# Down product by output quarters sorted by knots, with per-segment sums, in a decoder layer built from spline weights

## The chip, the cores and the metric

One NeuronCore of a Trainium2 chip runs the whole layer as one program. The metric is the device time of one execution in microseconds, the median over runs. The engines are TensorE (PE; its weight loads are shown as PEld), VectorE (DVE), ScalarE (ACT), GpSimd (POOL) and SyncE (SP, which issues DMAs here). TensorE has two clock levels, 1.2 and 2.4 GHz; a granted clock of 1.00 is 2.4 GHz.

## The reference

`x` is (8, 256, 512): 8 batches of 256 tokens. The layer is

```
x = layernorm(x + attention(x))           # 16 heads of 32, softmax, low-rank down/up per head
x = layernorm(x + x * scan(ctx * ctx))    # per head r = decay * r + ctx^2 along the tokens
gate, up = x @ gate_w.T, x @ up_w.T       # gate_w, up_w: (2048, 512)
x = layernorm(x + (silu(gate) * up) @ down_w.T)   # down_w: (512, 2048)
```

Each of the three feed-forward weights is a Catmull-Rom spline over a flat index: 8134 control points over 1,048,576 elements, so a knot falls every 128.9 elements. Between two knots the weight is a cubic polynomial of the flat index. Each output row of `down_w` has 2048 elements and thus some 16 knots.

## The kernel before, in words

**Precision.** Matmul operands are mostly fp32r. A value is split into a high part and a remainder (`hi`, `lo`), and one product is three matmuls: high x high, high x low, low x high (helper `three`, lines 303 to 305). Where an operand is plain f32, one call shows in the trace as two records.

**Attention part**, batch by batch (`pe_batch`, `act_batch`, `dve_batch`, `pool_batch`). For each of four groups `m` of four heads: `pe_s` makes the scores (line 478; each head uses 32 rows of the array and its own bank), DVE takes the maxima (`dve_max`, line 821), ACT the exponentials with their sums (`act_exp`, line 665), PE transposes them (`pe_t`, line 490), DVE and ACT copy them to SBUF (`probsT`, line 835), DVE inverts the sums and widens them (`dve_inverse`, lines 827 and 830), PE transposes those (`pe_r`, line 498), and `pe_pv` multiplies with V (line 512; each head writes its own 32 partitions). Between these PE does projections of the next batch. The order on PE is `pe_pv(m)`, then `pe_s(m + 1)`. The recurrence is a scan on DVE (`dve_scan`, line 896), after the copies of group 2, or in the last batch in two halves before the inverses of groups 2 and 3. `pe_extra` puts transposes of spline coefficients (batches 1 to 3) and jobs (batches 4 to 7) in between.

**Jobs.** A job makes one tile of weights from spline coefficients: `pe_job` (line 1096) multiplies makers (powers of the position) with coefficients for the piece before and the piece after a knot, ACT copies the first (`act_job`, line 1105), DVE overwrites it by mask with the second (`dve_job`, line 1117), ACT rounds the high part (line 1124), and GpSimd or DVE makes the low part (`pool_job_lo`, line 1132, `dve_job_lo`, line 1139). Sixteen jobs make gate and up in a basis of a few features per 128 inputs; 32 jobs of two matmuls (128 rows, 256 columns) make the whole down weight, `dn[g]`. Makers and masks come by GpSimd's DMA queue. The first `AHEAD_JOBS` run before the feed-forward part.

**Feed-forward part.** Four blocks `n` of 512 tokens; in each, 8 steps `g` (256 of the 2048 hidden units each), j = 0, 1 (128 units each). The inputs are first turned to features (`pe_xt`, transposes, line 1165; `pe_features`, line 1191; then ACT and DVE split them and SP's queue spreads them by group, line 1220). These run ahead for the next block as "turns" through the single bank `F`, three places in each step. `pe_gate_up` makes `G` and `U` (three matmuls of 512 columns each); `act_silu` (line 1356) reads `G`, `dve_hm` (line 1398) multiplies with `U`, `act_hh` (line 1369) rounds and `dve_hl` (line 1402) takes the remainder. Banks `G`, `U` and the tile `hidden` are single. `pe_down` multiplies the hidden values of the step before with `dn[g]`: for each of four tiles of 128 tokens, two `j` times three matmuls, summed over all 8 steps in banks 0 to 3. The order on PE in a step is written out by hand:

```
gate/up 0, turn 0, down 0, fill 0, down 1, fill 1, turn 1,
gate/up 1, fill 2, down 2, fill 3, turn 2, down 3
```

where the fills are the remaining jobs, in block 0 alone. After step 7 DVE adds the residual (`dve_add`, line 1408) and takes statistics (lines 1412, 1594), GpSimd the reciprocal root (lines 1638, 1640), DVE normalizes (`dve_out`, line 1426), and GpSimd issues the output DMAs (line 1482). ACT and DVE do their work of a step in a fixed order as well (`act_step`, `dve_step`): every engine takes its instructions in program order.

## Time and profile before

| | us |
|---|---|
| median of 3 runs (684.74 to 684.94) | 684.91 |
| the profiled execution | 685.51 |
| its span, first to last instruction | 683.7 |
| PE busy (4312 matmuls) | 656.8 (96%) |
| DVE busy | 449.5 (66%) |
| ACT busy | 347.7 (51%) |
| POOL busy | 294.3 (43%) |

The attention part ends at about 367, the first gate/up matmul starts at 376.7, the last matmul at 672.99. The duration of a single matmul includes the way through the array and overlaps with the next one; the spacing of the starts is what it costs PE. Idle time is that of the engine before the instruction named, and what released it.

### The profile page before, as it was taken

How to read it: one execution, taken by the hardware profiler on the slowest of the kernel's cores; microseconds unless marked ns; L12 is line 12 of the kernel's file. 1: busy time of each engine (PE TensorE's matmuls, PEld its weight loads, DVE VectorE, ACT ScalarE, POOL GpSimd, SP SyncE). 2: the span in 40 equal slices, each digit the busy share in tenths (PEclk: the TensorE clock that was granted, in tenths of full speed). 3: DMA queues.
4: the chain of work that ended last, by engine and by line, in shares of the span. 5: the costliest groups of instructions: out<-in, count | busy, mean ns of one | idle time of the engine just before them, and what ended most of it. 6: DMA issues, size and time to landing. Idle time of an engine off the chain costs nothing.

```text
span 683.7 us, 12025 instructions
## 1 busy us (share of the span) xinstructions
PE 656.8 (96%) x4312; PEld 533.8 (78%) x4312; DVE 449.5 (66%) x826; ACT 347.7 (51%) x1002; POOL 294.3 (43%) x351
## 2 busy tenths in 40 slices
PE   9999999999999999999988799999999999999993
PEld 9597887878888788788865577888888888888883
DVE  3567687698686877878778688666544555354434
ACT  5566546637466565656667556552334233333230
POOL 1764486886638767594674836100100001000103
PEclk9999999999999999999999999999999999999997
DMA  9621020030220311121112672741193317340301
GB/s 329 221 80 62 1 87 7 2 125 1 94 62 2 133 52 32 63 72 41 40 65 47 159 173 72 210 105 40 35 239 78 81 32 198 72 101 0 124 1 61
DMA packets 22010, 58.06 MB, mean 85 GB/s; under 512 B 4032, under 2 KB 7232, under 8 KB 21056
## 3 DMA queue, kind: packets, MB, share of 16 engines
q1 hardware_dynamic: 16720, 44.45, 22.5%
q0 software_dynamic: 4944, 12.32, 5.9%
q8 instruction: 35, 0.57, 0.3%
...
## 4 chain that ended last, share of the span: by engine, by line
PE 78%; DVE 12%; ACT 6%; issue 2%; POOL 1%; DVEq 0%; POOLq 0%; ACTq 0%
PE bank L303 19%; PE bank L305 18%; PE bank L304 18%; PE bank L490 6%; ACT probs L665 5%; PE bank L478 4%; DVE recurrence_T L896 4%; PE bank L512 4%; DVE minus_max L821 3%; PE bank L1191 2%; PE bank L1096 2%; DVE probsT L835 2%; PE bank L529 1%; PE bank L316 1%; PE bank L498 1%
## 5 line engine op out<-in xcount | busy, mean ns | idle before, releaser
L665 ACT ACTIVATE probs<-bank,minus_max 128x256 f32<-128x256 f32 x256 | 117.3, 486 | 23.8 <-DVE minus_max L821 23.8
L303 PE MATMUL bank<-down,hidden_hi_lo 128*128 128x512 f32 x256 | 100.7, 393 | 1.5 <-DVE hidden_hi_lo L1402 1.5
L305 PE MATMUL bank<-down,hidden_hi_lo 128*128 128x512 f32 x256 | 100.5, 392 | 0.0
L304 PE MATMUL bank<-down,hidden_hi_lo 128*128 128x512 f32 x256 | 100.0, 391 | 0.0
L821 DVE TENSOR_REDUCE minus_max<-bank 128x2 f32<-128x512 f32 x128 | 79.3, 681 | 16.3 <-PE bank L478 16.3
L1398 DVE TENSOR_TENSOR hidden<-bank,silu 128x512 f32<-128x512 f32 x64 | 44.1, 689 | 60.9 <-PE bank L305 58.9
L1356 ACT ACTIVATE silu<-bank 128x512 f32<-128x512 f32 x64 | 38.3, 598 | 82.2 <-PE bank L305 81.3
L1402 DVE TENSOR_TENSOR hidden_hi_lo<-hidden,hidden_hi_lo 128x512 fp32r<-128x512 f32 x64 | 45.5, 711 | 40.9 <-ACT hidden_hi_lo L1369 40.8
L490 PE MATMUL bank<-ident,probs 128*128 128x128 f32 x512 | 65.5, 275 | 6.2 <-ACT probs L665 5.9
L1476 POOL TENSOR_TENSOR ffn_var_eps<-ffn_mean_var,constants 128x4 f32<-128x4 f32 x3 | 0.6, 196 | 156.5 <-DVE ffn_mean_var L1418 156.5
L490 PEld LDWEIGHTS bank<-ident,probs 128*128 128x128 f32 x512 | 56.6, 141 | 14.2 <-ACT probs L665 12.0
L1369 ACT CAST hidden_hi_lo<-hidden 128x512 fp32r<-128x512 f32 x64 | 39.8, 622 | 52.3 <-DVE hidden L1398 52.3
L835 DVE COPY probsT<-bank 128x512 f32<-128x512 f32 x96 | 60.1, 680 | 4.8 <-PE bank L490 4.7
L303 PEld LDWEIGHTS bank<-down,hidden_hi_lo 128*128 128x128 f32 x256 | 48.1, 188 | 11.5 <-DVE hidden_hi_lo L1402 1.9
L305 PEld LDWEIGHTS bank<-down,hidden_hi_lo 128*128 128x128 f32 x256 | 48.0, 188 | 10.3
L665 ACT ACTIVATION_READ_ACCUMULATOR probs<-bank,minus_max 128x1 f32 x256 | 55.9, 219 | 0.0
L304 PEld LDWEIGHTS bank<-down,hidden_hi_lo 128*128 128x128 f32 x256 | 48.1, 188 | 9.7
L303 PE MATMUL bank<-xT_hi_lo,wq_hi 128*128 128x256 f32 x128 | 38.7, 303 | 1.1 <-DVE spline_coef_T_down L773 0.4
L303 PE MATMUL bank<-xT_hi_lo,wk_hi 128*128 128x256 f32 x128 | 38.9, 304 | 0.0
L512 PE MATMUL bank<-probsT,V 128*32 128x256 f32 x512 | 36.8, 385 | 0.4 <-ACT inverse_by_query L680 0.4
L478 PE MATMUL bank<-k_heads,q_heads 32*128 32x256 f32 x512 | 36.7, 400 | 0.0
L305 PE MATMUL bank<-xT_hi_lo,wq_lo 128*128 128x256 f32 x128 | 36.1, 282 | 0.0
...
## 6 DMA issues: line engine op xcount, KB each, us to landing
features_by_group<-features_by_cell SPq DMA_DIRECT2D x128, 128.0 KB, 2.4
...
```

The costliest lines, as they stand in the source:

```text
L303: nc.tensor.matmul(out, wh, xh, start=first, stop=False)
L304: nc.tensor.matmul(out, wh, xl, start=False, stop=False)
L305: return nc.tensor.matmul(out, wl, xh, start=False, stop=last)
L478: last = nc.tensor.matmul(S[g][:, t * T:(t + 1) * T], qk[0][at, m, t * P:(t + 1) * P], qk[1][at, m, :], start=True, stop=True)
L490: last = nc.tensor.transpose(S[g][:, kt * T + t * P:kt * T + (t + 1) * P], probs[:, g, t, kt * P:(kt + 1) * P], ident[:])
L512: last = nc.tensor.matmul(MI[g * DH:(g + 1) * DH, 0:T], V[:, kt, h * DH:(h + 1) * DH], probsT[:, g, kt, :], start=kt == 0, stop=kt == TT - 1)
L665: inc(nc.scalar.activation(probs[:, g, t, :], S[g][:, t * T:(t + 1) * T], ACT.Exp, bias=nmax[:, g, t:t + 1], accum_out=rsum[:, t, g:g + 1] ...
L821: inc(nc.vector.tensor_reduce(nmax[:, g, :], S[g][:].rearrange("p (t k) -> p t k", t=TT), AX.X, ALU.max, negate=True), "max")
L835: inc(nc.vector.tensor_copy(probsT[:, g, :, :], S[g][:].rearrange("p (k t) -> p k t", k=2)), "ptv")
L1369: inc(nc.scalar.copy(hid[:, g % 2, 0, j, :], hm[:]), "hh")
L1398: inc(nc.vector.tensor_tensor(hm[:], U[:], sg[:], ALU.mult), "hm")
L1402: inc(nc.vector.tensor_tensor(hid[:, g % 2, 1, j, :], hm[:], hid[:, g % 2, 0, j, :].bitcast(F32), ALU.subtract), "hl")
```

## The change

The down product is taken the other way round, with the outputs on the partitions of the banks and 512 tokens as columns. The 512 outputs are sorted by where their knots fall and cut into 4 quarters of 128; the 2048 hidden units are cut into 64 segments between knots, 16 for each quarter. For a quarter, the 512 hidden units of its own segments, where its knots lie, are multiplied with exact weights (`pe_raw`: 64 units of quarter 2 * pair on rows 0 to 63 and 64 of the next on rows 64 to 127, each with its own bank; one more such tile for two units that were moved between quarters). All other weights are cubic over each segment, so four sums per segment (`pe_moments`: of the hidden values times 1, k, k^2, k^3) times four coefficients give their share (`pe_polynomials`). The quarters' results are split and brought back to token rows and to the outputs' order by matmuls with a 0/1 matrix (`pe_place`). Steps are now `st`: steps 0 to 3 take hidden units of quarters 0 and 1, steps 4 to 7 of 2 and 3.

The down weights take 13 jobs instead of 32; a job is now 16 calls (the one for the moved units 32) in plain f32 with 64 stationary columns, 128 moving columns, into upper or lower partitions of banks 2 and 3 in turn. Four of them run ahead, nine in steps 0 to 3 of block 0. Turns, fills and the last steps get new places.

In the attention part the scores of the next group go ahead of the product with V, the maxima ahead of `dve_y`, `act_yh` into the middle of the exponentials; the widening of the inverse goes from DVE to ACT; the scan goes whole to before the inverse of group 2, and in the last batch behind the attention. At the end of the program ACT normalizes (a third small GpSimd step makes -mean * rstd) and SP issues the output DMAs.

The core of the diff (left out: the tables made on the host, buffers, semaphores, and edits that follow from these):

```diff
         if proj:
             pe_k(pe, nb, 1, rest)
         pe_extra(pe, b, 2)
+
+        pe_s(pe, b, 3)
         pe_pv(pe, b, 2)
-
-        pe_s(pe, b, 3)
         if proj:
             pe_v0(pe, nb)
             pe_v1(pe, nb, range(0, 2))
...
             pe.wait_ge(s_mkg[g % 2], 16 * (g // 2 + 1))
             by = [(mk_gu[g % 2][:, piece * P:(piece + 1) * P], splD[w][:, g, :]) for piece in range(2)]
         else:
-            g, k = divmod(i - 2 * NG, 2 * JT)
-            j, hf = divmod(k, 2)
-            pe.wait_ge(s_mkd[g % 2], 16 * (g // 2 + 1))
-            by = [(mk_dn[g % 2][:, j * P:(j + 1) * P], downD[:, j, piece, hf * GROUP:(hf + 1) * GROUP]) for piece in range(2)]
+            k = i - 2 * NG
+            pe.wait_ge(s_mkd[k % 4], 16 * (k // 4 + 1))
+            mk = mk_dn[k % 4][:].rearrange("p (c b h m) -> p c b h m", c=2, b=2, h=2).bitcast(F32)
+            for piece in range(2):
+                for cb in range(2):
+                    for b in range(2):
+                        q, terms = job_terms(k, cb, b, piece)
+                        o = out[b * PART:(b + 1) * PART, piece * GROUP + cb * P:piece * GROUP + (cb + 1) * P]
+                        for n, (of, coef) in enumerate(terms):
+                            for h in range(2):
+                                last = nc.tensor.matmul(o, mk[:, of, b, h, :], downD[:, h, coef, q * P:(q + 1) * P].bitcast(F32),
+                                                        start=n == h == 0, stop=h == 1 and n == len(terms) - 1)
+            inc(last, "w")
...
+    def pe_moments(pe, n, st):
+        pair, pr = divmod(st, Q)
+        pe.wait_ge(s["hl"], JT * (STEPS * n + st) + JT)
+        if pr == 0:
+            wait(pe, "mol", 2 * n + pair)
+            if n == st == 0:
+                wait(pe, "ws", AHEAD_JOBS)
+                pe.wait_ge(s["seg"], 16)
+        for h in range(2):
+            for j in range(JT):
+                last = nc.tensor.matmul(Mo[:], by_segment[:, JT * st + j, :], hid[:, st % 2, h, j, :],
+                                        start=pr == h == j == 0, stop=pr == Q - 1 and h == j == 1)
+        if pr == Q - 1:
+            inc(last, "mo")
+
+    def pe_raw(pe, n, st):
+        pair, pr = divmod(st, Q)
+        pe.wait_ge(s["hl"], JT * (STEPS * n + st) + JT)
+        if n == 0:
+            if st < 4:
+                pe.wait_ge(s["wl"], 2 * NG + st + 1)
+            else:
+                pe.wait_ge(s["wld"], STEPS - 3 if st == MOVED_STEP else st - 3)
+        for b in range(2):
+            q = 2 * pair + b
+            if pr == 0 and n == 0:
+                if pair == 0:
+                    wait(pe, "r1", 2 * B)
+                else:
+                    pe.wait_ge(s["ws"], NJOB)
+                    wait(pe, "rs1", 2 * B)
+            elif pr == 0:
+                wait(pe, "add", BT * (n - 1) + q + 1)
         for j in range(JT):
-            last = three(Dn[t][:], [hid[:, g % 2, h, j, t * P:(t + 1) * P] for h in range(2)], [dn[g][:, h, j, :] for h in range(2)],
-                         g == 0 and j == 0, g == NG - 1 and j == JT - 1)
-        if g == NG - 1:
-            inc(last, "d")
-        elif t == BT - 1:
-            inc(last, "hused")
-
-    OWN = {(1, 1): 4, (1, 2): 5, (2, 0): 6, (2, 1): 7}
-    AHEAD = {(2, 2): 0, (3, 0): 1, (3, 1): 2, (3, 2): 3, (4, 0): 4, (4, 1): 5, (5, 0): 6, (5, 1): 7,
-             (6, 2): 8, (7, 0): 9, (7, 1): 10, (7, 2): 11}
...
+            for k, (lo_w, lo_h) in enumerate(((0, 0), (0, 1), (1, 0))):
+                for b in range(2):
+                    rows_ = slice(b * PART, (b + 1) * PART)
+                    last = nc.tensor.matmul(Dn[2 * pair + b][:], raw[st][rows_, lo_w, j * P:(j + 1) * P],
+                                            hid[rows_, st % 2, lo_h, j, :], start=pr == j == k == 0, stop=False)
+        if st == MOVED_STEP:
+            for lo_w, lo_h in ((0, 0), (0, 1), (1, 0)):
+                last = nc.tensor.matmul(Dn[1][:], raw[STEPS][0:PART, lo_w, 0:P], hid[0:PART, st % 2, lo_h, 0, :],
+                                        start=False, stop=False)
+        inc(last, "hused")
+
+    def pe_polynomials(pe, n, pair, quarters_):
+        pe.wait_ge(s["mol"], 2 * n + pair + 1)
+        if n == 0:
+            wait(pe, "wld", STEPS + 1 - 4 + 2 * pair + 2)
+        for q in quarters_:
+            last = three(Dn[q][:], [by_poly[:, pair, h, q * P:(q + 1) * P] for h in range(2)], [mom[:, pair, h, :] for h in range(2)],
+                         False, pair == 1)
+            inc(last, "d" if pair else "kap")
+
+    def pe_place(pe, n, t):
+        wait(pe, "yll", Q * n + Q)
+        if n == t == 0:
+            pe.wait_ge(s["place"], 16)
+        for q in range(Q):
+            for h in range(2):
+                last = nc.tensor.matmul(Dn[t][:], yq[:, q, h, t * P:(t + 1) * P], places[:, q, :],
+                                        start=q == h == 0, stop=q == Q - 1 and h == 1)
+        inc(last, "pm")
+
+    OWN = {(0, 0): 4, (0, 1): 5, (0, 2): 6, (1, 0): 7}
+    AHEAD = {(1, 2): 0, (2, 0): 1, (2, 1): 2, (2, 2): 3, (3, 0): 4, (3, 1): 5, (3, 2): 6, (4, 0): 7,
+             (7, 0): 8, (7, 1): 9, (7, 2): 10, (8, 0): 11}
...
+    def turn_of(n, st, at):
+
+        if n == 0 and (st, at) in OWN:
+            return 0, BT + OWN[st, at]
+        if n and (STEPS + st, at) in AHEAD:
+            return n, AHEAD[STEPS + st, at]
+        if n < NB - 1 and (st, at) in AHEAD:
+            return n + 1, AHEAD[st, at]
+        return None
+
...
+    FILL = {0: (4, 5), 1: (6, 7), 2: (8, 9), 3: (10, 11, 12)}
+
+    def job_of(n, st, k):
+
+        return 2 * NG + FILL[st][k] if n == 0 and st in FILL and k < len(FILL[st]) else None
+
...
-    def pe_step(pe, n, g):
-        prev = before(n, g)
-        pe_gate_up(pe, n, g, 0)
-        pe_turn(pe, n, g, 0)
-        pe_down(pe, prev, 0)
-        pe_fill(pe, n, g, 0)
-        pe_down(pe, prev, 1)
+    def pe_step(pe, n, st):
+        prev = before(n, st)
+        pe_gate_up(pe, n, st, 0)
+        pe_turn(pe, n, st, 0)
+        if n and st == 1:
+            for t in range(BT):
+                pe_place(pe, n - 1, t)
         if prev:
-            pe_fill(pe, n, g, 1)
-        pe_turn(pe, n, g, 1)
-        pe_gate_up(pe, n, g, 1)
-        pe_fill(pe, n, g, 2 if prev else 1)
-        pe_down(pe, prev, 2)
-        pe_fill(pe, n, g, 3)
-        pe_turn(pe, n, g, 2)
-        pe_down(pe, prev, 3)
+            pe_moments(pe, *prev)
+            pe_fill(pe, n, st, 0)
+            pe_raw(pe, *prev)
+        else:
+            pe_fill(pe, n, st, 0)
+        pe_turn(pe, n, st, 1)
+        pe_fill(pe, n, st, 1)
+        pe_gate_up(pe, n, st, 1)
+        pe_fill(pe, n, st, 2)
+        if n and st == 0:
+            pe_polynomials(pe, n - 1, 1, range(Q))
+        if st == 6:
+            pe_polynomials(pe, n, 0, range(Q))
+        pe_turn(pe, n, st, 2)
 
...
-    def act_step(act, n, g):
-        act_silu(act, n, g, 0)
...
+    def act_step(act, n, st):
+        prev = before(n, st)
+        if n and st == 1:
+            for q in range(2):
+                act_outs(act, n - 1, q)
+        act_silu(act, n, st, 0)
+        if n and st == 1:
+            for q in range(2, Q):
+                act_outs(act, n - 1, q)
+        act_hh(act, n, st, 0)
+        act_turn(act, n, st, 0)
+        if prev and prev[1] % Q == Q - 1:
+            act_moments(act, prev[0], prev[1] // Q)
+        act_fill(act, n, st, 0)
+        act_turn(act, n, st, 1)
+        act_fill(act, n, st, 1)
+        act_fill_hi(act, n, st, 0)
+        act_silu(act, n, st, 1)
+        act_fill_hi(act, n, st, 1)
+        act_hh(act, n, st, 1)
+        act_fill(act, n, st, 2)
+        act_fill_hi(act, n, st, 2)
+        act_turn(act, n, st, 2)
 
...
+    def dve_outs(dve, n, q):
+        dve.wait_ge(s["yhh"], Q * n + q + 1)
+        inc(nc.vector.tensor_tensor(yq[:, q, 1, :], Dn[q][:], yq[:, q, 0, :].bitcast(F32), ALU.subtract), "yll")
+
     def dve_add(dve, n, t):
         if t == 0:
             dve.wait_ge(s["fres"], 16 * n + 16)
-        dve.wait_ge(s["d"], BT * n + t + 1)
+        dve.wait_ge(s["pm"], BT * n + t + 1)
         inc(nc.vector.tensor_tensor(res[:, t, :], Dn[t][:], res[:, t, :], ALU.add), "add")
 
...
             pe_o(pe, B - 1, 1)
             pe.wait_ge(s["ws"], 2 * NG + 2)
             pe_job(pe, 2 * NG + 2, X)
+            pe_rs(pe, B - 1, 0)
+            pe_rs(pe, B - 1, 1)
+            pe.wait_ge(s["ws"], 2 * NG + 3)
+            pe_job(pe, 2 * NG + 3, X)
             for n in range(NB):
-                for g in range(NG):
-                    pe_step(pe, n, g)
+                for st in range(STEPS):
+                    pe_step(pe, n, st)
+            pe_moments(pe, NB - 1, STEPS - 1)
+            pe_raw(pe, NB - 1, STEPS - 1)
+            pe_polynomials(pe, NB - 1, 1, range(Q))
             for t in range(BT):
-                pe_down(pe, (NB - 1, NG - 1), t)
+                pe_place(pe, NB - 1, t)
 
...
```

`dve_step` mirrors `act_step`. In `dve_batch` the calls are moved thus (in `act_batch` the calls of `act_yh` for groups 0 to 2 go):

```diff
         dve_extra(dve, b, 0)
         if post:
             dve_stats(dve, b - 1, 0)
         dve_inverse(dve, b, 1)
         dve_heads(dve, b, 1)
 
+        dve_max(dve, b, 2)
         dve_y(dve, b, 1)
-        dve_max(dve, b, 2)
         dve_extra(dve, b, 1)
-        if not proj:
-            dve_scan(dve, b, range(2))
+        if proj:
+            dve_scan(dve, b)
         dve_inverse(dve, b, 2)
         dve_heads(dve, b, 2)
-        if proj:
-            dve_scan(dve, b, range(KT))
-        else:
+
+        dve_max(dve, b, 3)
+        dve_y(dve, b, 2)
+        if not proj:
             dve_x2l(dve, 0, 0, B_)
             dve_x2l(dve, 0, 1, C_)
-
-        dve_y(dve, b, 2)
-        dve_max(dve, b, 3)
         dve_extra(dve, b, 2)
-        if post:
+        if post and proj:
             dve_size(dve, b - 1)
-        if not proj:
-            dve_scan(dve, b, range(2, KT))
         dve_inverse(dve, b, 3)
         dve_heads(dve, b, 3)
         if not proj:
             dve_x2l(dve, 0, 2, B_)
             dve_x2l(dve, 0, 3, C_)
+            dve_size(dve, b - 1)
         dve_y(dve, b, 3)
...
```

## Rows read from the trace of the kernel before

**Rows 1.** Stretches: us, busy us by engine, granted clock, DMA share, GB/s.

```profile
24.00:361.00 337.00, 327.92 (x2771) 265.88 (x2770) 255.15 (x479) 204.03 (x720) 226.74 (x248) 1.00 0.17 56
...
367.40:376.70 9.30, 9.28 (x46) 7.45 (x47) 6.50 (x15) 5.37 (x13) 2.73 (x6) 1.00 0.44 99
376.70:458.50 81.80, 77.70 (x364) 61.78 (x363) 61.48 (x121) 48.63 (x108) 33.69 (x43) 1.00 0.54 141
458.50:530.20 71.70, 71.70 (x322) 58.59 (x321) 37.03 (x62) 26.17 (x44) 4.01 (x7) 1.00 0.40 102
...
601.80:673.20 71.40, 71.40 (x313) 58.34 (x311) 32.88 (x58) 19.54 (x32) 5.20 (x11) 1.00 0.17 48
673.20:683.80 10.60, 0.18 (x1) 0.00 (x0) 4.16 (x9) 0.00 (x0) 4.65 (x9) 0.66 0.27 99
```

**Rows 2.** Matmul groups by form, 376.7 to 673.3: busy us, mean ns.

```profile
L303 PE MATMUL bank<-down,hidden_hi_lo 128*128 128x512 f32 x256 | 100.7, 393 | 1.5 <-DVE hidden_hi_lo L1402 1.5
...
L1096 PE MATMUL bank<-spline_coef_T_down,makers_out 128*128 128x256 f32 x60 | 12.5, 290 | 1.4 <-DVE weights_now L1117 1.4
```

**Rows 3.** One step of block 2 in order of time: start, us, engine.

```profile
588.46 0.60 ACT L1356 ACTIVATE silu<-bank 128x512 f32<-128x512 f32 x1 [2.08 <-PE bank L305]
...
588.72 0.40 PE L305 MATMUL bank<-features_by_group,weights_lo_up 128*128 128x512 f32 x1
...
589.15 0.69 DVE L1398 TENSOR_TENSOR hidden<-bank,silu 128x512 f32<-128x512 f32 x1 [2.06 <-PE bank L305]
...
589.88 0.62 ACT L1369 CAST hidden_hi_lo<-hidden 128x512 fp32r<-128x512 f32 x1 [0.82 <-DVE hidden L1398]
...
590.33 0.61 PE L1191 MATMUL bank<-x2T_hi_lo,moments 128*128 128x512 f32 x2
590.53 0.69 DVE L1402 TENSOR_TENSOR hidden_hi_lo<-hidden,hidden_hi_lo 128x512 fp32r<-128x512 f32 x1 [0.69 <-ACT hidden_hi_lo L1369]
...
590.98 0.59 ACT L1206 CAST features_by_cell<-bank 128x512 fp32r<-128x512 f32 x1 [0.48 <-PE bank L1191]
...
591.60 0.69 DVE L1211 TENSOR_TENSOR features_by_cell<-bank,features_by_cell 128x512 fp32r<-128x512 f32 x1 [0.37 <-ACT features_by_cell L1206]
```

**Rows 4.** Tiled matmuls between untiled ones, order of time, PE.

```profile
249.61 0.48 PE L1096 MATMUL bank<-spline_coef_T_gate,makers_hidden 128*128 128x256 f32 x2
250.02 1.12 PE L512 MATMUL bank<-probsT,V 128*32 128x256 f32 x16
251.07 1.15 PE L478 MATMUL bank<-k_heads,q_heads 32*128 32x256 f32 x16
252.15 0.39 PE L303 MATMUL bank<-xT_hi_lo,wq_hi 128*128 128x256 f32 x1
```

**Rows 5.** Plain f32 matmuls, untiled, order of time, PE.

```profile
10.98 3.74 PE L341 MATMUL bank<-recurrence_T,spline_coef_rows 128*128 128x128 f32 x32
14.47 0.36 PE L303 MATMUL bank<-xT_hi_lo,wq_hi 128*128 128x256 f32 x1
```

**Rows 6.** Steps 0 and 1 of block 0, order of time, PE.

```profile
383.61 0.40 PE L305 MATMUL bank<-features_by_group,weights_lo_up 128*128 128x512 f32 x1
385.49 0.49 PE L303 MATMUL bank<-down,hidden_hi_lo 128*128 128x512 f32 x1 [1.49 <-DVE hidden_hi_lo L1402]
```

**Rows 7.** Waits of PE in attention: total us, times, longest.

```profile
PE bank L490 <- ACT probs L665: 5.9, 19, 0.8
```

**Rows 8.** DVE in batch 5, order of time.

```profile
267.42 0.20 DVE L827 RECIPROCAL row_sum_inverse<-row_sum 128x8 f32<-128x8 f32 x1 [1.67 <-ACT probs L665]
...
270.26 4.88 DVE L896 TENSOR_TENSOR_SCAN recurrence_T<-decay,ctx_squared_T 128x256 f32<-128x256 f32 x4
```

**Rows 9.** The end, order of time.

```profile
672.99 0.39 PE L305 MATMUL bank<-down,hidden_hi_lo 128*128 128x512 f32 x1
...
674.89 0.68 DVE L1408 TENSOR_TENSOR x_residual<-bank,x_residual 128x512 f32<-128x512 f32 x1
...
677.65 0.55 DVE L1426 TENSOR_SCALAR x_residual<-x_residual,ffn_mean_var,ffn_rstd 128x512 f32<-128x512 f32 x1 [0.70 <-POOL ffn_rstd L1640]
```

599 lines of the change are left out of this document (356 added, 243 removed).

## The prediction

> **What bounds the kernel now.** I read the stretches first, then the matmul groups, one step in order of time, the waits, and the end. TensorE (PE) is the bound: of 337 us of attention it idles 9, in blocks 1 to 3 of the feed-forward part nothing, and the granted clock is 1.00 up to the end [rows 1]. Block 3 is the ruler: 71.40 us for 313 matmuls of 512 columns, back to back, 0.228 us each [rows 1]. Elsewhere PE waits in the first steps of block 0 (4.1 us of 81.8 [rows 1], the longest 1.49 us for the low half of the hidden values [rows 6]), on softmax in attention (5.9 us [rows 7]), and for the 10.6 us after the last matmul, when only VectorE, GpSimd and the output DMAs work [rows 1, 9]. So a change pays only by what it takes from PE's list, and costs whatever it puts there, waits included.
>
> **Step chain.** The chain behind each hidden tile, from the start s of the last `up` matmul (588.72) [rows 3]: silu starts at s-0.26, `hidden` s+0.43, high half s+1.16, low half s+1.81, ready at about s+2.53; silu releases `G` at s+0.39, `hidden` releases `U` at s+1.17. A turn (features or transposes through the one bank `F`) frees the bank 1.96 us after it begins: matmuls at 590.33, copy at 590.98, subtraction 591.60 to 592.29, if both engines are free. Before, two output tiles of the down product (12 matmuls, 2.7 us) stand between a step's second gate/up and the next step's first, and again behind that first; they hide this chain.
>
> **The change, PE's list per normal block.** Gone: 192 down matmuls. Added: 32 for `pe_moments`, 24 for `pe_polynomials`, 32 for `pe_place`, 3 for the moved units, and 96 half-height matmuls in `pe_raw`. These last alternate between rows 0 to 63 and 64 to 127 and between two banks. Row and column tiles at work [rows 4]: scores (32 rows, four tiles) and probabilities times V (32 columns, four tiles) do 16 records each in 1.05 and 1.08 us, against 32 records of 128 columns in 3.49 us untiled [rows 5], that is 0.109 each, 0.218 for 256 columns. Four tiles thus run nearly side by side. I count a pair of half-height matmuls as one of 0.228. fp32r in row tiles is not in this trace; the other end is no overlap, 0.456. So the list falls from 304 to 251 slots, 53 less, 12.1 us a block: 48.3 us in all.
>
> **Switches.** From the first untiled matmul of 249.61 to that of 252.15 pass 2.54 us. Its two L1096 matmuls take 0.24, the eight groups of four 8 x 0.218 = 1.74; 0.56 is left for three changes of tiling, 0.18 each [rows 4]. Every `pe_raw` has two, 32 of them: 64 x 0.18 = 11.5 us; the jobs (column tiles) add about 14 changes, 2.5 us. Bounds: nothing to 0.3 each (all of one group's latency).
>
> **New waits.** In the new `pe_step` all moments and raw work lies between gate/up 0 and gate/up 1; between gate/up 1 and the next step's moments lie only the 6 matmuls of the next gate/up and the turns. (a) No turns there (4 to 5, 5 to 6 in each block, and three more in block 3): PE reaches `G` at s+0.23, waits to s+0.39; `U` at s+1.08, waits to s+1.17; moments at s+1.85, wait to s+2.53. 0.9 us, eleven times: 10 us. (b) A turn before and one after that gate/up: the first turn's copy stands behind the high half on ScalarE and its subtraction behind the low half on VectorE, so bank `F` is free only at s+3.1, where PE asks at s+2.05. 1.05 us, twelve times (less with a fill between, more often shared with 0.2 in the turn before): 12 us. (c) `pe_place` wants all four quarters split high and low: after the last polynomial PE has 6 matmuls (1.4 us), the split of quarter 3 queues behind silu and `hidden` of the new step and ends 3.5 us after it: 2.1 us, three times. (d) In step 3 of blocks 1 and 2 the turn stands behind four statistics (2.4 us) of `dve_out_stats`: 2.1 us each. (e) At the end the low half (2.3) and the last split (1.6) are bare. Behind a waiting PE nothing else can go, and ScalarE and VectorE then wait for PE.
>
> **Jobs.** `pe_job` of the outputs was 2 matmuls of 256 columns, about 0.24 us (60 such records in the blocks [rows 2]). Now it is 16 calls in plain f32, 32 records of 128 columns at 0.109 [rows 5], in two column tiles; side by side 1.74, with start and drain 1.95 us; one after another 3.5. What decides between the ends [rows 4]: there too a tile's own records come one after the other and the four tiles still run together. Twelve such jobs, one of double length, for 32 old ones.
>
> **Blocks.** Blocks 1 and 2: 203 full matmuls 46.3, 48 pairs 10.9, 16 transposes 1.7, 16 switches 2.9, waits 2.1 + 2.1 + 1.8 + 4.2 = 10.2: 72.0, with gate/up's slower 0.231 about 72.3, against 71.7. Block 0: 161 matmuls 36.7, 42 pairs 9.6, transposes 1.7, ten job lengths 19.5, 28 switches 5.0, waits 7: 79.5; I add 1.5, since its job waits before were never quite what the chain says: 81.0 against 81.8. Block 3 up to the last matmul, with two blocks' worth of placing and three of polynomials' groups: 237 matmuls 54.0, 54 pairs 12.3, switches 3.2, waits 2.1 + 4.5 + 2.3 + 1.6 = 10.5, and 1 for gate/up's pace: 81.0 against 71.4. Sum: -0.8 + 1.2 + 9.6 = +10.
>
> **Bridge** (367.4 to 376.7, 9.3 us [rows 1]): four jobs with switches, 4 x 2.3 = 9.2, for three of 0.24 to 0.5; the rest stays, and the scan of the last batch (4.8 us [rows 8]) is hidden by the output projection. +8.
>
> **Attention.** Scores move ahead of the product with V, so the maxima begin 1.05 us earlier; the scan goes ahead of the inverse. PE's softmax waits (5.9 [rows 7]) may go. But the scan starts near 265.1 instead of 270.26 and lasts 4.8 (270.26 to 275.07), where VectorE had 1.67 us free [rows 8]: the inverse, ready at 267.42, comes at 269.9, and ScalarE's wide copy and PE's `pe_r` wait 0.6 us for it. In batches 0 to 6 that gives back most: -3 in all, with the projection's wait at batch 0. In batch 7 no scan is left and two phases shorten: -3.3. Together -6.3; bounds -12 (all 9.1 of PE's idle time in the stretch, and some 2 to 3 behind it) and +3 (nothing gained, 0.6 lost in five batches).
>
> **End.** Before: last matmul 672.99, span 683.7, 10.7 us; VectorE lagged, its last add came 1.9 us behind the matmul, and GpSimd issued four DMAs at the end [rows 9]. After: placing (8 matmuls, 1.8 us) paces the adds, the add follows at +0.42, statistics and mean +1.45, GpSimd's three small steps 1.3, ScalarE 0.9 with its wait, SyncE's DMA and the end about 3.5 (before, 5.5 from the last normalization to the end with four DMAs issued in a row by GpSimd): 7.7. -3.
>
> Sum: -6.3 + 8 + 10 - 3 = +8.7 on the span 683.7, 692.4; 1.8 us lie around the span (685.51), and the median of the runs is 0.6 below that execution: **693.5 us**. Makers, masks and `places` come over GpSimd's queue a step or more ahead; `pool_norm2` of batch 6 delays makers 8 to 11 by 7 us, used from step 2, 18 us on: nothing. The extra evacuations on ScalarE and VectorE (six of 0.6 to 0.7 us a block) fit: both are under 55% busy in block 1 [rows 1]. Features' DMAs keep their distance of two steps.
>
> **The order of tiles.** For the jobs it matters in which order tiles may start [rows 4]. There, 16 records of 0.218 in four column tiles take 1.05 us, though each call is two records on its own tile. Were every record to start in the program's order, the second record of one call would hold back the next tile's first, and the product with V would need 9 x 0.218 = 1.96 us. It does not; so I let the two tiles of a job run side by side. The Trainium skill ("TensorE: Matmul & The Clock Gate", on packing small matmuls, what overlaps and what doesn't) says instead that matmuls start and end strictly in program order. By that rule the sum would be that of rival 2; the trace speaks against it.
>
> **Rivals.**
> 1. *Changing the tiling costs nothing where PE's queue is full* (it is paid within a wait). 86 switches less: -15.4, 678. For it: switches beside waits may share them. Against: [rows 4], where the queue was full and 0.56 us are missing. It decides from 0.08 us a switch downward.
> 2. *Job records in strict order.* A job is four times eight records, four on one tile and then four on the other; in strict order only the last of the one lies beside the first of the other, 6 x 0.109 instead of 4, so 2.7 in place of 1.95, fourteen lengths: +10.5, 704. No overlap at all: 3.5, +21.7, 715. For it: four records in a row on one tile are deeper than the two of [rows 4].
> 3. *Row pairs don't overlap in fp32r*: 192 x 0.228 less 3 us of waits hidden, +41, 734. Against: [rows 4], where the scores write four banks at once at a column every two cycles each, the same total.
> 4. *The waits at step ends are smaller*, or attention gives its whole 12 us: 684 to 689, no change or a little slower.
>
> **Chances.** My forecast 0.55, its own range 688 to 700. Rival 1 0.20, rival 2 0.12 and 0.04, rival 3 0.04, rival 4 0.05. A measurement tells 0.2% (1.4 us) from no change. Faster: rival 1 and a little of 4 and of attention, 0.25; within, 0.07; slower 0.68. Range 679 to 706: it leaves out no overlap, about 0.1, and the edge of rival 1.
>
> **What would show it.** Blocks 1 and 2 of 72 us in place of 71.7, with PE busy about 90% instead of 100%. PE idle before `moments` behind the low half (0.7 us, eleven times), before turns behind `features_by_cell` or `x2T` (1 us), before placing 2 us. A raw burst of 12 records in 1.4 to 1.6 us; 2.7 would be rival 3. A job of 32 records in 2.0; 3.5 would be rival 2. Weight loads "issue" 0.3 us at each change of tiling. In attention the transposes of head group 3 without waits and `pe_r` of group 2 with 0.6. The prediction fails if switches are free, if the jobs don't pair, or if the attention part shortens by over 9 us.

## The result, and the profile after

The changed kernel takes **706.03 us** (median; 699.7 to 707.1), the kernel before 684.92 us on the same chip: a ratio of 1.0287, 95% interval 1.0225 to 1.0349. It is slower, by 21.1 us where 8.6 were forecast. The profiled execution took 705.22 us, its span is 703.3 us.

The same stretches as in [rows 1], now of the kernel after: us, busy us (and instructions) of TensorE (PE), its weight loads, VectorE (DVE), ScalarE (ACT), GpSimd (POOL), then the granted clock, DMA share and GB/s. They are attention, the bridge, blocks 0 to 3, and the end.

```profile
24.00:356.20 332.20, 325.09 (x2802) 268.62 (x2801) 232.13 (x452) 218.86 (x766) 229.03 (x254) 0.99 0.19 62
356.20:381.00 24.80, 20.27 (x168) 16.26 (x169) 12.12 (x24) 6.45 (x15) 10.24 (x15) 0.86 0.57 136
381.00:462.50 81.50, 75.12 (x584) 56.08 (x582) 44.16 (x78) 32.82 (x66) 31.73 (x43) 1.00 0.40 102
462.50:538.80 76.30, 67.60 (x316) 47.49 (x315) 39.97 (x68) 28.06 (x50) 5.96 (x9) 0.98 0.49 128
538.80:612.40 73.60, 66.02 (x317) 46.45 (x316) 40.07 (x68) 27.95 (x50) 3.98 (x7) 1.00 0.36 94
612.40:697.10 84.70, 76.31 (x346) 52.67 (x344) 42.64 (x73) 27.81 (x48) 6.12 (x14) 0.98 0.18 50
697.10:703.30 6.20, 0.00 (x0) 0.00 (x0) 1.57 (x3) 1.78 (x3) 1.95 (x6) 0.85 0.34 128
```

Against [rows 1]: attention ends 11.2 us earlier (its first feature matmul starts at 356.2 instead of 367.4), the bridge is 15.5 us longer, block 0 0.3 shorter, blocks 1 and 2 4.7 and 2.0 longer, block 3 13.1 longer, and from the end of the last matmul to the end of the span pass 6.2 us instead of 10.3. Together +19.6 on the span. The reader sees two things at once. PE was busy for all of blocks 1 to 3 before; now it is busy for about 90%. And the granted clock, 1.00 before in every stretch but the end, is now below 1.00 in four of the six stretches ahead of the end.

The waits of PE in the four blocks, total us, times, longest; before there were none in blocks 1 to 3:

```profile
PE bank L1346 <- DVE features_by_cell L1366: 10.1, 11, 1.7
PE bank L1463 <- DVE outs_hi_lo L1627: 7.4, 4, 2.0
PE bank L1413 <- DVE hidden_hi_lo L1619: 6.7, 12, 2.2
PE bank L1320 <- DVE x2T_hi_lo L1333: 3.1, 3, 1.0
PE bank L1346 <- DVE x2T_hi_lo L1333: 2.2, 3, 0.9
```

L1346 and L1320 are turns (features, transposes), L1463 is the placing, L1413 the moments. These are waits (a) to (e) of the prediction. With one of 1.0 us for the tables of a job (makers_out) there are 34, 30.5 us in all; the prediction had 37.9.

One step of block 3 in order of time, PE, start and us:

```profile
667.69 1.20 PE L1413 MATMUL bank<-hidden_hi_lo,by_segment 128*128 128x512 f32 x4 [0.42 <-DVE hidden_hi_lo L1619]
668.81 1.66 PE L1440 MATMUL bank<-hidden_hi_lo,down_raw 64*128 64x512 f32 x12
670.41 0.50 PE L440 MATMUL bank<-features_by_group,spline_coef_T_gate 128*128 128x512 f32 x1
670.75 0.39 PE L441 MATMUL bank<-features_by_group,spline_coef_T_gate 128*128 128x512 f32 x1
670.98 0.40 PE L442 MATMUL bank<-features_by_group,weights_lo_gate 128*128 128x512 f32 x1
```

Twelve half-height matmuls take 1.60 us from their first to the next gate matmul: the pairs do run side by side. A change of tiling has two parts here: the first matmul of the new kind comes 0.32 us after the last of the old (670.41 is 0.32 behind the last pair) instead of 0.23, and the one behind it 0.34 (670.41 to 670.75) instead of 0.23. Together 0.20 us. The weight loads of the same three matmuls show where the second part comes from:

```profile
670.41 0.19 PEld L440 LDWEIGHTS bank<-features_by_group,spline_coef_T_gate 128*128 128x128 f32 x1 [0.37 <-issue]
670.51 0.19 PEld L441 LDWEIGHTS bank<-features_by_group,spline_coef_T_gate 128*128 128x128 f32 x1
670.75 0.19 PEld L442 LDWEIGHTS bank<-features_by_group,weights_lo_gate 128*128 128x128 f32 x1
```

In a full stream the load of the next matmul begins together with the matmul before it (670.75). Here the first matmul's own load begins at 670.41, with the matmul, and the second's only at 670.51, 0.10 us late. The Trainium skill names a cause for the first part ("TensorEngine Tiling (Array Packing)", Tiling Modes): a change of the tiling mode, other than of the tile, makes TensorE drain first. The trace gives the price; whether the array is empty at 670.41 it cannot tell, since the ends of matmuls are modelled.

The placing of block 0's outputs, at 475.59 in order of time, and under it the windows of two half-clock stretches:

```profile
473.22 0.39 PE L442 MATMUL bank<-features_by_group,weights_lo_up 128*128 128x512 f32 x1
475.59 5.76 PE L1463 MATMUL bank<-spline_coef_T_down,outs_hi_lo 128*128 128x512 f32 x17 [1.99 <-DVE outs_hi_lo L1627]
```

```profile
476.10:479.50 3.40, 3.40 (x9) 2.66 (x9) 0.51 (x2) 0.00 (x0) 0.00 (x0) 0.51 1.03 216
626.30:629.70 3.40, 3.40 (x10) 2.62 (x9) 0.69 (x1) 0.00 (x0) 0.00 (x0) 0.51 0.00 0
```

PE stands still for 2 us, and right behind it the clock is at its lower level (1.2 of 2.4 GHz) for 3.4 us, in which about 8 matmuls start instead of 15: 1.6 us lost. It happened behind two of the three placings between blocks; the third, a wait of 1.98 us at 551.9, was followed by none, nor was the longest wait for the low half, 2.16 us at 682.4. Three more such stretches begin at 349.9 us, in attention's last batch, behind a wait of 2.5 us for transposed inputs, and at 360.1 and 377.2 us in the bridge, the one behind a wait of 1.95, the other within one of 2.54. So, from 24 us on, five of the seven waits of 1.9 us and more brought one.

### The profile page after: what moved, and what is told of

Read it like the earlier page. It is cut to its first block, busy times and chain, and to the rows that moved or that the text cites. A ratio compares the mean times of both kernels' runs of the same rounds, so it can differ in the third digit from the quotient of the medians.

```text
span 703.3 us, 12746 instructions
## 1 busy us (share of the span) xinstructions
PE 652.1 (93%) x4676; PEld 507.4 (72%) x4676; DVE 421.6 (60%) x775; ACT 356.2 (51%) x1024; POOL 297.8 (42%) x364
## 4 chain that ended last, share of the span: by engine, by line
PE 79%; DVE 12%; ACT 5%; DMA 2%; issue 1%; POOL 1%; DVEq 0%; ACTq 0%; POOLq 0%
PE bank L440 13%; PE bank L442 12%; PE bank L441 11%; PE bank L627 8%; PE bank L1440 7%; PE bank L615 5%; PE bank L1463 5%; PE bank L1413 4%; PE bank L649 4%; PE bank L1249 3%; DVE hidden L1615 3%; DVE hidden_hi_lo L1619 3%; ACT hidden_hi_lo L1574 3%; PE bank L1346 2%; ACT probs L804 1%
## 5 line engine op out<-in xcount | busy, mean ns | idle before, releaser
L804 ACT ACTIVATE probs<-bank,minus_max 128x256 f32<-128x256 f32 x256 | 118.8, 487 | 39.7 <-DVE minus_max L966 39.5
L627 PE MATMUL bank<-ident,probs 128*128 128x128 f32 x512 | 63.1, 277 | 1.1 <-ACT probs L804 1.1
L627 PEld LDWEIGHTS bank<-ident,probs 128*128 128x128 f32 x512 | 58.6, 143 | 4.2 <-ACT probs L804 1.8
L1440 PE MATMUL bank<-hidden_hi_lo,down_raw 64*128 64x512 f32 x384 | 53.1, 408 | 0.0
L1440 PEld LDWEIGHTS bank<-hidden_hi_lo,down_raw 64*128 64x128 f32 x384 | 33.7, 184 | 16.6 <-issue 10.8
L1059 POOL TENSOR_TENSOR yT_lo<-heads_out,yT_hi 128x256 fp32r<-128x256 f32 x24 | 19.9, 831 | 57.6 <-ACT yT_hi L812 57.6
L1413 PE MATMUL bank<-hidden_hi_lo,by_segment 128*128 128x512 f32 x128 | 36.2, 404 | 6.7 <-DVE hidden_hi_lo L1619 6.7
L1463 PE MATMUL bank<-spline_coef_T_down,outs_hi_lo 128*128 128x512 f32 x128 | 33.5, 424 | 7.4 <-DVE outs_hi_lo L1627 7.4
L1346 PE MATMUL bank<-x2T_hi_lo,moments 128*128 128x512 f32 x64 | 23.0, 445 | 15.0 <-DVE features_by_cell L1366 10.1
L1463 PEld LDWEIGHTS bank<-spline_coef_T_down,outs_hi_lo 128*128 128x128 f32 x128 | 26.0, 205 | 14.8 <-DVE outs_hi_lo L1627 9.0
L442 PE MATMUL bank<-xT_hi_lo,wq_lo 128*128 128x256 f32 x128 | 36.2, 283 | 0.0
```

Of the source, the lines that this page charges most:

```text
L442: return nc.tensor.matmul(out, wl, xh, start=False, stop=last)
L627: last = nc.tensor.transpose(S[g][:, kt * T + t * P:kt * T + (t + 1) * P], probs[:, g, t, kt * P:(kt + 1) * P], ident[:])
L804: inc(nc.scalar.activation(probs[:, g, t, :], S[g][:, t * T:(t + 1) * T], ACT.Exp, bias=nmax[:, g, t:t + 1], accum_out=rsum[:, t, g:g + 1] ...
L1413: last = nc.tensor.matmul(Mo[:], by_segment[:, JT * st + j, :], hid[:, st % 2, h, j, :], start=pr == h == j == 0, stop=pr == Q - 1 and h = ...
L1440: last = nc.tensor.matmul(Dn[2 * pair + b][:], raw[st][rows_, lo_w, j * P:(j + 1) * P], hid[rows_, st % 2, lo_h, j, :], start=pr == j == k ...
L1463: last = nc.tensor.matmul(Dn[t][:], yq[:, q, h, t * P:(t + 1) * P], places[:, q, :], start=q == h == 0, stop=q == Q - 1 and h == 1)
```

## Experiments

All times are medians of four executions; ratios are to the kernel before, run on the same chip (its medians there: 685.0, 686.0 and 685.1 us). The change itself was not run beside them: what is said to be less or more than the change compares with the 706.03 above, so differences of 1 us mean nothing there. Where intervals of ratios overlap, the profiled executions decide.

**1. The attention part alone.** The kernel before with the change's attention edits; the last batch's scan and transposes of the recurrence behind the output projection, as in the change.

```
before:  pe_pv(b, m-1); pe_s(b, m)          now:  pe_s(b, m); pe_pv(b, m-1)
before:  dve_y; dve_max; inverse; scan      now:  dve_max; dve_y; scan; inverse
bridge:  + dve_scan(B-1) behind job 16, pe_rs(B-1) behind the last job, pool_scaled(B-2) ahead of the jobs' low parts
```

> The kernel before with the change's attention part alone (scores ahead of the product with V, the evictions and the scan in their new places); its feed-forward part and its jobs are those of before. Theory: the attention part ends some 11 us earlier (356.2 instead of 367.4 us in the trace of after) and nothing behind it takes that back, since the jobs of the bridge are short again: 673 to 677 us, a ratio near 0.985. Rival: the last batch's scan and the size chain, now behind the attention part, hold up the bridge, and at least half of it is given back: 679 to 684 us.

677.84 us, ratio 0.9892 (0.9877 to 0.9907): faster than before by 7.2 us. Attention ends at 356.1 us, as in the change, and the bridge takes 13.0 us instead of 9.3. So some 4 of the 11.3 us are given back there: the scan, the size chain and the transposes now lie in the bridge, and a half-clock stretch of 3.4 us begins at 360.0. Another begins at 349.8, as in the change; the kernel before has neither. The gain in the whole is nearly the 6.3 of the forecast, and the time lies between what the two theories named.

**2. Twice the changes of tiling.** The change, with moments and row pairs each cut in two.

```
-  moments(4 matmuls); raw(12)
+  moments(h=0: 2); raw(j=0: 6); moments(h=1: 2); raw(j=1: 6)
```

> After, with the moments of a step cut in two: two matmuls, the first half of the row pairs, the other two matmuls, the second half. The same matmuls in number and size, 62 more changes between whole matmuls and row pairs. Theory (a change of tiling costs 0.18 to 0.2 us of TensorE): +11 to +13 us, a ratio of 1.016 to 1.018. Rival (a change of tiling is free and what the trace shows there belongs to waits): within 1 us of after.

715.43 us, ratio 1.0442 (1.0421 to 1.0463). In the profiled executions the span grows by 9.3 us, with four half-clock stretches ahead of the end against five, so by 10.9 at the same clock. The edit makes 64 more changes of tiling, two in each of 32 steps (143 in the blocks instead of 79), not the 62 I had counted: 0.17 us for each. PE's waits in the blocks shrink by 1.6 us, so some of the price falls into them; a change with no wait beside it costs the 0.20 above. Second matmuls that come 0.31 to 0.37 us after the first rise from 127 to 186. The growth is just under the 11 to 13 of the theory; the rival (free) falls, and with it rival 1 of the prediction.

**3. Another order within a step.**

```
-  gate/up 0; turn 0; [place]; moments(prev); raw(prev); turn 1; gate/up 1; [polynomials]; turn 2
+  gate/up 0; moments(prev); turn 0; gate/up 1; turn 1; [place]; raw(prev); [polynomials]; turn 2
```

The copies and subtractions of turn 1 and the four additions follow behind the second hidden tile on ScalarE and VectorE; the splits of the moments go ahead of turn 0's.

> After, with the work of a step in another order: the moments directly behind the first gate/up, the placing, the row pairs and one turn behind the second gate/up, so that each wait has other matmuls ahead of it. The same matmuls, the same number of changes of tiling. Theory (a large part of the loss in the blocks is waiting that the order causes; by the durations of the trace the waits shrink from 17 to some 2 us, and the drops of the clock behind them go too): 15 to 22 us less than after, 684 to 691 us. Rival (the loss is in the switches and the exposed weight loads, which stay): at most 5 us less, 701 us or more.

681.44 us, ratio 0.9949 (0.9931 to 0.9968): 24.6 us less than the change with the same matmuls and 75 changes of tiling in the blocks in place of 79, and now faster than before. Its blocks:

```profile
378.20:461.60 83.40, 75.59 (x583) 59.39 (x582) 46.45 (x79) 34.16 (x67) 33.88 (x45) 0.96 0.40 104
461.60:530.20 68.60, 65.20 (x316) 48.11 (x315) 40.00 (x67) 28.57 (x50) 4.13 (x7) 0.98 0.54 142
530.20:599.10 68.90, 65.28 (x316) 47.86 (x315) 39.90 (x67) 28.35 (x50) 3.99 (x7) 0.98 0.38 100
599.10:672.90 73.80, 71.24 (x346) 52.73 (x344) 42.10 (x72) 27.65 (x47) 6.18 (x14) 1.00 0.19 55
```

Blocks 1 and 2 fall below the 71.7 of before. The waits for hidden_hi_lo go from 6.7 us (12 times) to 0.6 (once), those of the placing from 7.4 to 1.4. Block 0 is 1.9 us longer than in the change: a wait of 3.7 us for the tables of the last job, one of 2.4 for a turn, and a half-clock stretch with each. The drops of the clock did not go, as the theory had it: there are five ahead of the end, as in the change. So the 24 us between the two profiled executions (680.87 at a mean clock of 0.985, 705.22 at 0.987) are not the clock's; most of them are waits. Two of the five come in blocks 1 and 2, where no wait is longer than 1.02 us, behind two such waits 2 us apart:

```profile
495.46 0.50 PE L440 MATMUL bank<-features_by_group,spline_coef_T_up 128*128 128x512 f32 x1 [0.92 <-DVE hidden L1614]
497.44 0.73 PE L1346 MATMUL bank<-x2T_hi_lo,moments 128*128 128x512 f32 x2 [1.00 <-DVE features_by_cell L1366]
```

```profile
498.20:501.70 3.50, 3.50 (x14) 2.38 (x15) 1.29 (x2) 0.93 (x2) 0.00 (x0) 0.51 0.00 0
```

The other is at 566.5 us, behind waits of 0.93 and 1.02.

**4 and 5. One piece of that order each.** First only the row pairs behind the second gate/up, then only the placing (with the row pairs of that step and the additions).

```
4:  -  moments(prev); raw(prev); turn 1; gate/up 1        5:  -  [place]; moments; raw; turn 1; gate/up 1
    +  moments(prev); turn 1; gate/up 1; raw(prev)            +  moments; turn 1; gate/up 1; [place]; raw   (step 1 only)
```

> After, with one thing of the new order alone: the row pairs of a step behind the second gate/up instead of ahead of it. Theory (the wait for the second gate/up and the one for the low part at the step's end shrink when matmuls stand between them; the placing still waits): 6 to 10 us less than after, 696 to 700 us. Rival (the gain of the new order lies in the moments, turns and placing): within 3 us of after, 703 us or more.

699.29 us, ratio 1.0200 (1.0161 to 1.0238; the top of it touches the change's interval): 6.7 us less than the change. The waits for the low half fall from 6.7 to 0.6 us, but the turns' for features_by_cell rise from 10 to 14, and the clock is worse (mean 0.979, with half-clock stretches from 377 us on at 377.7, 428.9, 500.6, 551.8 and 579.1 us, the third of double length).

> After, with the placing alone (and the row pairs that wait for it, and the four additions on VectorE) behind the second gate/up of step 1 instead of behind the first, three times in the kernel. Theory (2.0 us of waiting each, and the clock's drop behind two of them, go once other matmuls stand ahead): 6 to 9 us less than after, 697 to 700 us. Rival (the chain of the second gate/up is then bare, since nothing stands between the two gate/up groups but the moments): 1 to 3 us less.

690.12 us, ratio 1.0065 (1.0048 to 1.0082): 15.9 us less than the change by the medians, twice what I expected. The spans of the profiled executions differ by 14.5, of which 12.6 lie in blocks 1, 2 and 3:

```profile
460.60:530.90 70.30, 65.57 (x317) 46.38 (x316) 40.10 (x68) 28.29 (x50) 5.92 (x9) 1.00 0.53 138
530.90:601.40 70.50, 65.61 (x316) 46.41 (x315) 40.04 (x68) 28.28 (x50) 3.98 (x7) 1.00 0.37 98
601.40:682.60 81.20, 75.24 (x346) 52.77 (x344) 42.60 (x73) 27.95 (x48) 6.12 (x14) 0.98 0.18 52
```

6.0, 3.1 and 3.5 us less. Step 1 of each gave 3.9, 2.3 and 4.3 (the wait of 2.0, the restart, and the half clock where there was one), step 2 0.9, 0.9 and 0.7 (a wait less), and step 7 of block 1 1.1; step 7 of block 3 lost 1.5 to a half-clock stretch at the wait of 2.16, which brought none in the change. The bridge, which the edit does not touch, is 1.6 us shorter, because its wait of 2.54 brought no half-clock stretch this time. That part is luck. The piece that costs most in the change is still where it places. The two pieces together give 22.6 of the 24.6 us of experiment 3; its other moves (the moments, turn 1) no run tests alone.

**6. PE kept busy during one wait.** The change, with eight matmuls more, whose result is not used, ahead of the placing between blocks.

```
+  wait(pe, "fl", NFT * (n + 1))
+  for k in range(8): nc.tensor.matmul(F[:], splD[0][:, 0, 0:P], feat[:, 0, 0, :], ...)
   for t in range(BT): pe_place(pe, n - 1, t)
```

> After, with eight more matmuls of 512 columns (8 x 0.228 = 1.8 us; their result is not used) in each of blocks 1 to 3 ahead of the placing, where TensorE stands still for 2 us. Theory (the drops of the granted clock come from TensorE standing still): the stretches at the half level at 476 and 626 us are gone and the rest stays, 1 to 4 us less than after, 702 to 705 us. Rival (the drops have nothing to do with the wait): they stay, and the time is that of after or up to 1 us more.

701.83 us, ratio 1.0245 (1.0210 to 1.0281). That interval and the change's overlap, so the time alone shows no gain; the trace is the evidence. The same two places:

```profile
474.00:482.00 8.00, 8.00 (x39) 6.35 (x39) 2.77 (x4) 0.00 (x0) 0.00 (x0) 1.00 0.59 121
612.00:630.00 18.00, 17.83 (x86) 13.93 (x84) 8.88 (x14) 4.49 (x9) 0.00 (x0) 1.00 0.27 60
```

No stretch at the half level is left between 362 us and the end of the matmuls. Part of that is chance: the bridge's wait of 2.5 us and the one of 2.16 in block 3 are left as they were, and none came at those either. What speaks for the theory is the placing: in the traces of the change and of experiments 2, 4 and 9, seven of its twelve waits of 1.98 to 1.99 us were followed by a half-clock stretch, here none of the three that were filled. The other three executions had mean clocks of 0.990, 0.994 and 0.987 against 0.997 here, so there the clock was lower somewhere; they have no profile. The useless work of 1.8 us in three places cost nothing: at the same mean clocks (0.994 and 0.987) this kernel took 699.6 and 704.4 us, the change 699.7 and 705.2.

**7 and 8. A wait put into the kernel before**, where nothing else waits: in step 5 of blocks 1 to 3 PE waits behind the first gate/up, once for the low half of that step's hidden tile, once for the tile itself.

```
    pe_gate_up(pe, n, g, 0)
7:  + if n and g == 5: pe.wait_ge(s["hl"], JT * (NG * n + g) + 1)
8:  + if n and g == 5: pe.wait_ge(s["hm"], JT * (NG * n + g) + 1)
```

> The kernel before, with one wait more in step 5 of blocks 1, 2 and 3: TensorE waits behind the first gate/up for the low half of the hidden values of that same step. By the step chain the low half is ready 2.5 us behind the start of the last up matmul, so TensorE stands still for some 2.3 us, three times. Theory (standing still for that long also brings the granted clock down to its half level for 3.4 us, 1.6 us each in the change's trace): 3 x (2.3 + 0.1 + 1.6) = +12 us, 697 us, with three stretches at the half level. Rival (a wait costs its own length): +7 us, 692 us, clock 1.00.

695.67 us, ratio 1.0149 (1.0125 to 1.0173), +10.5. Blocks 1 to 3 of the profiled execution, and the stretch behind the second of the three waits:

```profile
457.70:531.80 74.10, 71.94 (x321) 58.47 (x320) 37.09 (x62) 26.32 (x44) 4.03 (x7) 1.00 0.39 99
531.80:607.50 75.70, 73.54 (x321) 59.60 (x320) 37.07 (x62) 26.31 (x44) 4.11 (x7) 0.98 0.36 91
607.50:681.60 74.10, 71.91 (x313) 58.30 (x311) 33.18 (x58) 19.57 (x32) 5.44 (x11) 1.00 0.16 47
580.20:583.80 3.60, 3.60 (x10) 2.78 (x10) 0.69 (x1) 0.59 (x1) 0.00 (x0) 0.53 0.45 94
```

```profile
577.12 0.40 PE L305 MATMUL bank<-features_by_group,weights_lo_up 128*128 128x512 f32 x1
579.68 0.73 PE L1191 MATMUL bank<-x2T_hi_lo,moments 128*128 128x512 f32 x2 [2.16 <-DVE hidden_hi_lo L1404]
580.25 0.58 PE L303 MATMUL bank<-down,hidden_hi_lo 128*128 128x512 f32 x1
580.63 0.63 PE L304 MATMUL bank<-down,hidden_hi_lo 128*128 128x512 f32 x1
```

Three equal waits of 2.16 us. Two cost 2.5 us each (74.1 against 71.6), one cost 4.1, and only behind that one the clock fell. So the theory was right in kind and too strict: such a wait can bring the clock down, it need not. The four executions took 693.7, 695.6, 695.7 and 697.9 us at mean clocks of 0.993, 0.990, 0.990 and 0.985, about 2 us a step, as if one, two, two and three waits had; only the first of them has a profile, and the kernel before itself took 684.8 to 686.2 us on this chip.

> The same, with the wait for the hidden values before they are split, which are ready 1.2 us behind the start of the last up matmul: TensorE stands still for some 0.9 us, three times. Theory (waits of that length, as the change has at many steps, cost their length and the exposed weight load and leave the clock alone): 3 x (0.9 + 0.1) = +3 us, 688 us. Rival (they bring the clock down as well): +8 us, 693 us.

689.01 us, ratio 1.0049 (1.0034 to 1.0064), +3.9. The wait is 0.78 us each, the clock stays at 1.00 in the blocks, and each block is 1.1 us longer (72.7 against 71.6): a wait costs 0.3 us more than the profile says of it. One of the three, and the matmuls around it:

```profile
576.76 0.40 PE L305 MATMUL bank<-features_by_group,weights_lo_up 128*128 128x512 f32 x1
577.94 0.73 PE L1191 MATMUL bank<-x2T_hi_lo,moments 128*128 128x512 f32 x2 [0.78 <-DVE hidden L1400]
```

The profile counts the wait from the end of the last matmul, 0.39 behind its start, where the next would have started at 0.23; and the second matmul after it comes 0.33 instead of 0.23 later. The one half-clock stretch of this execution ahead of the end is in attention, at 364.1 us, behind a row of waits of which the longest are 0.80 and 1.04 us.

**9. The bridge.** The change, without what stands between PE's jobs on VectorE: the size chain and bn_stats of batch 6.

```
-  dve_size(B-2) ahead of the last product with V's eviction;  dve_stats(B-2, 1) between jobs 17 and 18
+  dve_size(B-2) behind job 19;                                dve_stats(B-2, 1) at the end of step 0
-  pool_scaled(B-2) behind job 17's low part                   + behind job 19's
```

> After, with the size chain of batch 6 moved behind the last job of the bridge, its scaling in GpSimd's queue behind the jobs' low parts, and its bn_stats into the first step of block 0. Theory (two of TensorE's waits in the bridge, 1.95 and 2.54 us, stand behind these instructions on VectorE, and the clock's drop at 377 us follows the second one): 3 to 6 us less than after, 700 to 703 us. Rival (other work of the bridge ends as late, the waits only change their names): within 1.5 us of after.

698.72 us, ratio 1.0214 (1.0165 to 1.0262), 7.3 us less than the change. Its bridge:

```profile
355.90:373.50 17.60, 17.22 (x168) 13.56 (x168) 9.11 (x16) 6.44 (x15) 6.24 (x10) 1.00 0.81 179
```

17.6 instead of 24.8 us: the waits of 1.95 and 2.54 are gone, and the two half-clock stretches of the bridge as well. That is more than the 3 to 6 I expected, since I had put only one of the two stretches down to these waits. (The intervals of this ratio and of the change's overlap, as its clock varies too; the bridge's row is the evidence.)

**10. All of it.** The new order, the bridge's edit, the last table ahead of the normalization in GpSimd's queue, and a finished block's four bn_stats in twos behind steps 2 and 4.

> The new order of the steps and the bridge's edit together, the last part of the tables for the jobs fetched ahead of batch 7's normalization in GpSimd's queue, and the bn_stats of a finished block spread over steps 2 and 4 instead of four at the end of step 2. Theory (the gains of the two earlier runs add up, the wait of 3.7 us for the tables goes, and in step 3 the waits of 1.9 us and the drop of the clock behind them go too): 681.4 - 7.3 - 3.7 - 1.6 - 2 to 5 = 664 to 669 us. Rival (each wait is replaced by the next in the queue): 672 to 676 us.

664.38 us, ratio 0.9680 (0.9662 to 0.9697). (One of its four executions took 1568.4 us, which nothing in its records explains; it is left out of the ratio. The others took 663.0, 663.5 and 665.3, median 663.45.) That is at the lower end of the 664 to 669 of the theory: the gains add up. Blocks 1 and 2:

```profile
453.20:518.80 65.60, 63.24 (x317) 47.17 (x315) 40.10 (x67) 28.57 (x50) 4.13 (x7) 1.00 0.53 137
518.80:584.60 65.80, 63.27 (x316) 47.22 (x315) 40.01 (x67) 28.37 (x50) 3.98 (x7) 1.00 0.42 103
```

**11. Four jobs whole.** The same with the four jobs by moment as 8 matmuls with all 128 output rows in fp32r instead of 32 records in half tiles; their table is stored in that order.

> The kernel of the run before this one, with the last four jobs (down's weights by moment) made of 8 whole matmuls of 128 columns in fp32r instead of 32 records of plain f32 in half tiles. Theory (the jobs cost TensorE 2.0 us each and a change of tiling on both sides): 4 x (2.0 - 0.5 to 1.8) + 4 to 8 changes x 0.2 = 2 to 7 us less than that run. Rival (the jobs' steps wait for the evictions of the jobs anyway): within 1 us of it.

662.70 us, ratio 0.9656 (0.9638 to 0.9673), 1.7 less than the run before, or 0.8 less than the median of its other three; the intervals overlap, so the time alone is no evidence. In the profiled executions block 0 falls from 79.4 to 76.9 us, though a half-clock stretch at 422 us, which the run before did not have there, is in it. At like mean clocks (0.997 and 0.998) it took 660.5 us against 663.0 and 663.5. So some 2.5 to 3 us, the low end of what I expected.

## Why the prediction was wrong

The direction was right, the list of matmuls, the pairs, the jobs and the changes of tiling too. The size was not: +19.6 on the span against +8.7.

- **Attention, -6.3, measured -11.2:** mis-sized, and past the 9 us that the prediction gave as a sign of its failing. It put -3 on batches 0 to 6 and -3.3 on batch 7; by the first scores of batch 7 (316.0 us instead of 326.4) 10.5 of the gain had already come, and the 0.6 us by which `pe_r` was to wait there does not show in the profile's waits. Batches 1 to 6 are where the waits for the exponentials went: by the start times the transposes of the probabilities lose 5.6 us less there. Batch 7 has a new wait of 2.5 us for transposed inputs and a half-clock stretch with it. In the whole kernel the edit alone gives -7.2 (experiment 1), since the bridge gives back 3.7 of it; that this is near 6.3 is in part luck.
- **Row pairs, one slot of 0.228 a pair:** right; 12 in 1.60 us. Rival 3 is out. The Trainium skill ("TensorE: Matmul & The Clock Gate", Packing small matmuls, the mechanism) gives some 4 ns between the starts of neighbouring tiles, and the records of a pair start 3 to 4 ns apart.
- **Jobs, 1.95 us:** right; 1.95 from the first start to the next matmul (372.10 to 374.05), so neither the 2.7 of rival 2 nor its 3.5. Four jobs in the bridge showed it: two lasted 2.02, and two at or partly at the half clock 3.13 and 3.39.

```profile
361.19 3.13 PE L1249 MATMUL bank<-spline_coef_T_down,makers_out 128*64 128x128 f32 x32
...
372.10 2.02 PE L1249 MATMUL bank<-spline_coef_T_down,makers_out 128*64 128x128 f32 x32
374.05 1.09 PE L666 MATMUL bank<-ident,recurrence_T 128*128 128x128 f32 x8
377.68 3.39 PE L1249 MATMUL bank<-spline_coef_T_down,makers_out 128*64 128x128 f32 x32 [2.54 <-DVE weights_now L1275]
```

- **Bridge, +8, measured +15.5: the step that failed is "the rest stays".** The scan was hidden (VectorE did it in 2.93 us from 365.11, while PE did the output projection). But I costed the jobs and no wait. Two VectorE steps stood in the jobs' way: the size chain (1.95 us, at 359.4), and bn_stats of batch 6, which waits for GpSimd's scaling of `residual_even`. That was queued behind two jobs' low parts and four DMA issues:

```profile
371.31 0.56 POOL L1301 DMA_DIRECT2D makers_out<-in_makers_out  x1
371.87 0.55 POOL L1302 DMA_DIRECT2D masks_out<-in_masks_out  x1
372.45 3.12 POOL L1110 TENSOR_SCALAR residual_even<-residual_even,scale 128x512 f32<-128x512 f32 x2
```

```profile
374.07 0.70 DVE L938 BATCH_NORM_STATS2 bn_stats<-residual_even 128x6 f32<-128x512 f32 x1 [3.96 <-POOL residual_even L1110]
375.60 0.69 DVE L938 BATCH_NORM_STATS2 bn_stats<-residual_even 128x6 f32<-128x512 f32 x1 [0.84 <-POOL residual_even L1110]
```

  The mask of job 18 comes behind them on VectorE, and job 19 on PE waits for that. Experiment 9 takes both out and gets 7.2 us of the 7.5 back: 4.5 are the two waits, the rest is mostly the clock with them.
- **Blocks, +10, measured +19.4: two costs are missing from the step "Blocks".** (1) The clock: I wrote it down as 1.00 and asked nothing further, though the change brings PE's first waits of 2 us into the blocks. 2 x 1.6 = 3.2 us (experiment 7 gives the price of one). (2) The restart: I priced a wait by its length alone, but behind it a second matmul comes 0.10 us late. By the start times in the trace that is 3.3 us behind the 34 waits that the profile lists, and 1.8 behind 18 shorter ones (a matmul 0.16 to 0.28 us late) that it does not list. The other terms held. The waits: 37.9 us foreseen; 30.5 by the profile, 36.2 counted from the start that was due, 39.7 with the 18 short ones. The changes of tiling: 78 and 14.0 us foreseen; 79, of which the 74 with no listed wait beside them took 14.4. That makes 3.2 + 3.3 + 1.8 + 1.8 + 0.4 = 10.5 for the 9.4 missing; the matmuls themselves took 1.1 less than I gave them.
- **End, -3:** measured -4.1. The last additions followed the placing without a lag, and the four normalizations on ScalarE kept that pace, as foreseen. Mis-sized is the last piece: from the last normalization (ends at 700.87) to the end of the span pass 2.4 us, where I put 3.5.

The rivals: changes of tiling are not free, jobs and pairs overlap, and of rival 4 the smaller waits are out for the change as written, while attention did give nearly its whole 12 us; the bridge and the blocks took more than that back. What I did not see is that the waits are no price of the idea, only of the order: experiment 3 keeps every matmul and all but four of the changes of tiling, and is 24.6 us faster. The 53 slots a block that the change saves are real: 12.1 us by the prediction, of which experiment 10 keeps 6.1 in block 1 (65.6 us in place of the 71.7 of [rows 1]) after some 3 us for the changes of tiling and some more for the waits that are left. The places where the next step's inputs are bare had eaten them.

Left open: which of two equal waits is followed by a lower clock, since of three of 2.16 us one was. What the clock does behind waits of 1 us that lie close together was seen in two traces (experiments 3 and 8) and not tested.
